# Reordered DMA issues and scatter calls in a cross-attention and mixture-of-experts kernel on one Trainium2 core

## The chip, the cores and the metric

The kernel runs on one core of one Trainium2 chip. The metric is the device time of one execution in microseconds (us); lower is better. The engines of the core run beside each other, each its own list of instructions: TensorE (PE) multiplies, VectorE (DVE), ScalarE (ACT) and GpSimd (POOL) work element by element, and SyncE (SP) issues most of the DMA transfers. Waits between them are semaphores.

## The reference, cut to what matters

```python
def reference(x, ctx, Wq, bq, Wk, bk, Wv, bv, Wo, bo, W_experts, b_experts, W_router, b_router):
    # x: (4, 2048, 512), ctx: (4, 154, 512), 16 heads of 32, 8 experts, the best 2 used
    h = layernorm(x)
    q, k, v = h @ Wq.T + bq, ctx @ Wk.T + bk, ctx @ Wv.T + bv
    attn = softmax(q k^T / sqrt(32))              # per head, 154 keys
    x = x + (attn @ v) @ Wo.T + bo
    h = layernorm(x)
    w = softmax(h @ W_router.T + b_router)        # only the two largest of the 8 kept
    return x + sum_e w[e] * (h @ W_experts[e].T + b_experts[e])
```

## The kernel before, in words

The 8192 tokens are worked on in 16 blocks of 512 (`NB` is 16). For a block b the attention stage does, in this order: normalize x (`NX`), transpose it (`XT`), project the queries (`Q`), copy them into a layout by head (the restack, `RS`), multiply them with the keys to find the largest score of each row (`MX`, 11 steps, `DMX` reduces them), send that row of maxima to the copy (`MT`, `MR`), multiply again with the maxima subtracted (`ST`, 10 steps), take exponentials (`EX`), split them into a high and a low half-precision part (`PH`, `PL`), multiply with the values (`PV`, 8 steps of which the last, number 7, ends the block), normalize and transpose (`NM`, `AT`), project (`O`), add to x (`BX`, `Oe`), compute the router (`LA`, `LB`, `RB` to `RW`) and scatter the normalized rows to a table in memory sorted by expert (`S1`, or `SC` and `SD` for blocks near the end; eight scatters of 128 rows for each block). After it comes the expert stage: 135 tiles of 128 rows are loaded from that table, multiplied with the weights of one expert each, and added to the output.

The attention stage is a software pipeline that is written out by hand. Each engine has a function of one slot (`pe_slot`, `act_slot`, `dve_slot`, `pool_slot`, `sp_slot`) that calls the steps of several blocks in a fixed order; slots run one after the other, in a loop in the middle of the stage and written out at its ends. Each engine works in order: a step that waits holds up all behind it.

SP's slot for block b issues the load of x for the residual (`XR`, block b-2), the keys (`K`, one DMA), the restack (`RS`, 12 DMAs of 128 KB from the `qs` buffers to `Qst`), the values (`V`, two DMAs), a piece of expert weights to convert (`WL`), the x of block b+3 (`XA`), the converted weights' store (`WW`), the row of maxima (`MR`) and the store of the residual (`XS`, block b-2). `K` and `RS` wait until `ST` of block b-2 is done (`stp`), `V` until `PV` of block b-2 is done (`pvt`), `RS` also until the queries' low part is there (`qle`). `MX` of the block waits for the restack and for the keys:

```python
        if n == 0:
            e.wait_ge(restack[p], b.half(192, 192))
            e.wait_ge(ld_k[p], b.half(16, 16))
```

All of SP's DMAs go through one queue (q1 in the profile), ACT's through a second (q10), POOL's indirect ones through a third (q0). Several buffers share one tensor and show by its name in the trace: `qs`, `Qst`, `Pst` and part of `xnT` are pieces of `we_s`, the buffers of `XA` are pieces of `be_s`, and `xn1` and `xn2` both show as `xn`. So the restack is `we_s<-we_s` (line 1312), `XA` is `be_s<-in_x` (1284), `XR` is `xR_s<-in_x` (1333), `WL` is `wst<-in_weT` (1350). On POOL, `PL` is line 1170, `BX` line 1246, a scatter `S1` line 1260, and a scatter of `SC` or `SD` line 1250.

In ACT's part, `act_EX` for the last block (15) also starts the loads of the expert weights into `we_s` (1 MB for each expert) and of the experts' biases (`be_s`, 2 MB), as soon as the buffers that lie there are no longer in use: three experts and the biases before step 5, two more experts after step 9. The other three are issued by SP after the attention stage.

Of the kernel before, what the change touches and what calls it, by code (L numbers as in the profile page):

```python
# [110 lines left out]
def build(nc, x, ctxT, wqT, bq, wkT, bk, wvT, bv, woT, bo, weT, be, wrT, br, wo, boc, out):  # L111
# [15 lines left out]
    def hold(e):  # L127

        e.sem_inc(tick[id(e)], 1)  # L129
# [132 lines left out]
    def s_(name):  # L262
        return sem(name, a)
# [22 lines left out]
    stp, exd, phd, pldp, pldd = s_("stp"), s_("exd"), s_("phd"), s_("pldp"), s_("pldd")  # L286
    pvt, rcd, nmd = s_("pvt"), s_("rcd"), s_("nmd")
# [606 lines left out]
    def load_experts(e, first, last):  # L894

        if last == NE:
            e.wait_ge(pvt, 8 * NB)
        e.wait_ge(st_we, 32 * last)
        for n in range(first, last):
            e.dma_start(we_s[:, n * WN:(n + 1) * WN], we_d[n].rearrange("p l k n -> p (l k n)")).then_inc(ld_ew, 16)  # L900

    def act_EX(e, b, n):
        if b.last and n == 5:
            e.wait_ge(qp, 4 * NB)
            e.wait_ge(lap, NB)
            e.wait_ge(restack[(NB - 1) % 2], 192 * NB // 2)
            e.wait_ge(stp, 10 * (NB - 1))
            e.wait_ge(nap[0], NJ * NB)
            load_experts(e, 0, 3)
            e.dma_start(be_s[:, :], be.rearrange("(a e) n -> a (e n)", a=1).broadcast_to([P, NE * D])).then_inc(ld_ew, 16)  # L910
        e.wait_ge(stp, b.at(10, n + 1))
        h = BANK[f"ST{n}"] - 2
        at = S[:, 2 * h:2 * h + 2, :]
        if n in PLP:
            i = PLP.index(n)
            if i >= R32 or b.past(1):
                e.wait_ge(pldp, b.at(NP, i - R32 + 1 if i >= R32 else (NP - 1 - i) // R32 * R32 + i - NP + 1))
            e.activation(P32[i % R32][:, :, :], at, ACT.Exp, scale=1.0 / (SS * ROOT)).then_inc(exd, 1)  # L918
        else:
            e.activation(at, at, ACT.Exp, scale=1.0 / (SS * ROOT)).then_inc(exd, 1)  # L920
        if b.last and n == 9:
            load_experts(e, 3, 5)
# [244 lines left out]
    def pool_PL(e, b, n):  # L1167
        e.wait_ge(phd, b.at(10, n + 1))
        r = 2 * (n % 5)
        e.tensor_tensor(Pst[1][:, r:r + 2, :], exps(n), Pst[0][:, r:r + 2, :], ALU.subtract).then_inc(pldp, 1)  # L1170
# [82 lines left out]
    def pool_S1(e, b, n):  # L1253
        p, k, j = b.par, n // NJ, n % NJ
        if n == 0:
            e.wait_ge(ridx, b.at(1, 1))
            e.wait_ge(rwd, b.at(RWD, RWD))
            e.wait_ge(nap[1], b.at(NJ, NJ))
            hold(e)
        e.indirect_dma_start(xs_d.ap(), bass.IndirectOffsetOnAxis(ap=idx[p][:, n:n + 1], axis=0),  # L1260
                             xn2[p][:, j, :], None).then_inc(scat[p][k], 16)
# [21 lines left out]
            hold(e)  # L1283
        e.dma_start(xA[b.par][:, :, :], blk_rows(x, b)).then_inc(ld_xA[b.par], 16)

    def sp_K(e, b):
        p = b.par
        if b.past(2):
            e.wait_ge(stp, b.at(10, -10))
            hold(e)  # L1290
        bt = b.c // 4 if b.reg is None else (b.reg * 2 + b.c) // 4
        if b.first:
            e.wait_ge(p_kd, 16 * 12)
        e.dma_start(Kst[p][0:96, :, :].rearrange("p (g G) c -> p g (G c)", g=4), k_d[:, :, bass.ds(bt, 1), :].rearrange("p g o n -> p (g o) n")).then_inc(ld_k[p], 16)

    def sp_V(e, b):
        bt = b.c // 4 if b.reg is None else (b.reg * 2 + b.c) // 4
        if b.past(2):
            e.wait_ge(pvt, b.at(8, -8))
            hold(e)  # L1300
            sp_values(e, b, bt)

    def sp_values(e, b, bt):
# [10 lines left out]
    def sp_RS(e, b):  # L1314
        if b.reg is None and b.c == 1:
            wait_values_stored(e)
        e.wait_ge(qle, b.at(4, 4))
        hold(e)
        if b.past(2):
            e.wait_ge(stp, b.at(10, -10))  # L1320
            hold(e)
        restack_heads(e, b, (0, 1) if b.first else range(4))
# [30 lines left out]
    def sp_WW(e, b):  # L1353
        e.wait_ge(wel, b.at(1, 1))
        hold(e)
        e.dma_start(we_d[bass.ds(expert_of(b), 1), :, :, 2 * (b.c % 2):2 * (b.c % 2) + 2, :].rearrange("o p l k n -> (o p) l (k n)"),
                    wsp[:, :, :]).then_inc(st_we, 16)
# [307 lines left out]
    def pool_slot(e, s):  # L1665
        bm2, bm1, b, bp1, bp2, bp4 = s + (-2), s + (-1), s, s + 1, s + 2, s + 4
        on_bm2, on_bm1, on_b, on_bp1, on_bp2, on_bp4 = bm2.here(), bm1.here(), b.here(), bp1.here(), bp2.here(), bp4.here()
        early1, early2 = on_bm1 and bm1.here(EARLY - 2), on_bm2 and bm2.here(EARLY - 2)
        if on_bp1:
            pool_PL(e, bp1, 2)  # L1670
        if early2:
            pool_S1(e, bm2, 4)
        if on_bm1 and not bm1.last:
            pool_RP(e, bm1)
        if on_bp1:
            pool_PL(e, bp1, 3)
        if on_b:
            pool_BX(e, b, 0)
        if on_bp1:
            pool_RC(e, bp1)  # L1680
        if on_b:
            pool_BX(e, b, 1)
        if early2:
            pool_S1(e, bm2, 5)
        if on_b:
            pool_BX(e, b, 2)
        if on_bm1 and not bm1.last:
            pool_RW(e, bm1)
        if on_bp1:
            pool_PL(e, bp1, 5)  # L1690
        if early2:
            pool_S1(e, bm2, 6)
        if on_bp4:
            pool_NC(e, bp4, 0)
        if early2:
            pool_S1(e, bm2, 7)
        if on_bp1:
            pool_PL(e, bp1, 7)
        if early1:
            pool_S1(e, bm1, 0)  # L1700
        if on_bp1:
            pool_PL(e, bp1, 8)
        if early1:
            pool_S1(e, bm1, 1)
        elif on_bm1 and bm1.here(NB - 3):
            pool_SC(e, bm1)
        if on_b:
            pool_BX(e, b, 3)
        if early1:
            pool_S1(e, bm1, 2)  # L1710
        if on_b and not b.last:
            pool_NC(e, b, 1)
            pool_RQ(e, b)
        if early1:
            pool_S1(e, bm1, 3)
        elif on_bm1 and bm1.here(NB - 3):
            pool_SD(e, bm1)
        if on_bp2:
            pool_PL(e, bp2, 0)

    def sp_slot(e, s):
        bm2, b, bp1, bp3 = s + (-2), s, s + 1, s + 3
        on_bm2, on_b, on_bp1, on_bp3 = bm2.here(), b.here(), bp1.here(), bp3.here()
        if on_bm2 and not bm2.last:
            sp_XR(e, bm2)
        if on_b:
            sp_K(e, b)
            sp_RS(e, b)
            sp_V(e, b)
        if on_bp1:  # L1730
            sp_WL(e, bp1)
        if on_bp3 and bp3.past(3):
            sp_XA(e, bp3)
        if on_b:
            sp_WW(e, b)
            sp_MR(e, b)
        if on_bm2 and not bm2.last:
            sp_XS(e, bm2)
# [381 lines left out]
```

## Time and profile before

| what | value |
|---|---|
| median of 3 runs | 1271.63 us (1269.0 to 1271.68) |
| time of the profiled execution | 1271.68 us |
| its span in the trace | 1270.0 us |
| mean granted TensorE clock | 0.977 of full speed |
| PE busy | 94% of the span |
| DVE, ACT, POOL busy | 69%, 56%, 59% |
| DMA | 239.19 MB, mean 188 GB/s |

The span is what the trace covers; the execution's time is 1.7 us more. Busy shares are averages over two stages with different limits: the attention stage lasts until about 830 us, the expert stage from there to the end. In rows of the trace the first number is a start in us after the span's start, the second a duration in us.

### The profile page before, as it was taken

How to read it: one execution, taken by the hardware profiler on the slowest of the kernel's cores; microseconds unless marked ns; L12 is line 12 of the kernel's file. 1: busy time of each engine (PE TensorE's matmuls, PEld its weight loads, DVE VectorE, ACT ScalarE, POOL GpSimd, SP SyncE). 2: the span in 40 equal slices, each digit the busy share in tenths (PEclk: the TensorE clock that was granted, in tenths of full speed). 3: DMA queues.
4: the chain of work that ended last, by engine and by line, in shares of the span. 5: the costliest groups of instructions: out<-in, count | busy, mean ns of one | idle time of the engine just before them, and what ended most of it. 6: DMA issues, size and time to landing. Idle time of an engine off the chain costs nothing. (4 is left out here: it accounts for less than half of the span.)

```text
span 1270.0 us, 35737 instructions
## 1 busy us (share of the span) xinstructions
PE 1192.7 (94%) x11024; PEld 719.1 (57%) x11025; DVE 873.1 (69%) x1933; ACT 717.4 (56%) x1040; POOL 745.0 (59%) x980
## 2 busy tenths in 40 slices
PE   7977999999999999999999988689899999999997
PEld 4444666666666666666666654444455555555554
DVE  3666798889888888988987876445455555555554
ACT  4327757966976786697687547233333333343333
POOL 4004337767866866776786578655645454554445
PEclk9979999999999999999999989789999999999999
DMA  9754535855765675586557448868999999898886
GB/s 249 223 166 119 142 127 159 245 168 188 229 197 191 197 223 184 173 255 181 194 170 219 153 140 303 312 151 206 200 178 177 176 189 180 168 183 165 159 165 127
DMA packets 135544, 239.19 MB, mean 188 GB/s; under 512 B 18439, under 2 KB 49415, under 8 KB 134279
## 3 DMA queue, kind: packets, MB, share of 16 engines
q1 hardware_dynamic: 102503, 161.24, 43.0%
q0 software_dynamic: 29808, 67.73, 26.4%
q10 hardware_dynamic: 3120, 8.68, 2.0%
q8 instruction: 76, 1.25, 0.4%
q14 instruction: 37, 0.30, 0.1%
HBM read 112.00 MB, written 101.40 MB: 168 GB/s over the span
## 5 line engine op out<-in xcount | busy, mean ns | idle before, releaser
L1902 PE MATMUL S<-we_s,wq_s 128*128 x1620 | 375.3, 382 | 13.2 <-DVE wq_s L1858 5.6
L1830 POOL DMA_INDIRECT out<-xn,to x135 | 208.8, 1547 | 209.4 <-DMA out<-xn,to 135.6
L1902 PEld LDWEIGHTS S<-we_s,wq_s 128*128 128x128 f16 x1620 | 157.6, 98 | 180.7 <-issue 21.8
L1170 POOL TENSOR_TENSOR we_s<-P_s,we_s 128x1024 f16<-128x1024 f32 x96 | 204.7, 2134 | 93.6 <-ACT we_s L936 92.8
L1841 ACT ACTIVATE wq_s<-PVp 128x512 f16<-128x512 f32 x137 | 81.6, 597 | 269.2 <-PE PVp L1892 243.7
L984 DVE TENSOR_REDUCE mx_sb<-S 128x6 f32<-128x924 f32 x160 | 171.4, 1112 | 11.9 <-PE S L726 8.9
L1880 DVE SCALAR_TENSOR_TENSOR att<-S,be_s 128x512 f32<-128x512 f32 x135 | 93.4, 692 | 108.8 <-PE S L1902 100.6
L746 PE MATMUL W<-wo_s,aT_hi 128*128 128x512 f16 x512 | 164.8, 384 | 3.0 <-issue 1.7
L708 PE MATMUL W<-we_s,wq_s 128*128 128x512 f16 x512 | 160.0, 384 | 4.4 <-DVE xnT_lo L962 3.6
L1858 DVE TENSOR_TENSOR wq_s<-PVp,wq_s 128x512 f16<-128x512 f32 x137 | 94.6, 691 | 39.1 <-ACT wq_s L1841 32.4
L818 PE MATMUL PVp<-Vm,we_s 128*128 128x33 f16 x3072 | 118.7, 178 | 0.2
L1260 POOL DMA_INDIRECT dispatched<-xn,idx x96 | 98.9, 1030 | 21.6 <-issue 19.9
L936 ACT ACTIVATE we_s<-P_s 128x1024 f16<-128x1024 f32 x96 | 102.2, 1065 | 8.6 <-PE PVp L818 4.7
L726 PE MATMUL S<-Kst,we_s 96*128 96x154 f16 x1024 | 99.3, 233 | 7.6 <-DVE mx_sb L984 5.3
L818 PEld LDWEIGHTS PVp<-Vm,we_s 128*128 128x128 f16 x3072 | 106.0, 97 | 0.4 <-issue 0.4
L726 PEld LDWEIGHTS S<-Kst,we_s 96*128 96x128 f16 x1024 | 78.8, 99 | 46.0 <-DVE mx_sb L984 8.0
L1094 DVE TENSOR_TENSOR we_s<-S,we_s 128x1024 f16<-128x1024 f32 x64 | 78.1, 1220 | 36.6 <-ACT we_s L936 36.6
L1848 ACT ACTIVATE xn<-att,wt 128x512 f32<-128x512 f32 x135 | 96.3, 713 | 9.8 <-DVE att L1880 3.8
L918 ACT ACTIVATE P_s<-S 128x1024 f32<-128x1024 f32 x96 | 98.4, 1025 | 2.4 <-PE S L786 2.4
L746 PE MATMUL W<-wo_s,aT_lo 128*128 128x512 f16 x256 | 98.4, 384 | 0.0
L708 PE MATMUL W<-xnT_lo,wq_s 128*128 128x512 f16 x256 | 98.2, 384 | 0.0
L815 PE MATMUL PVp<-Vr,we_s 128*128 128x132 f16 x768 | 87.3, 223 | 3.6 <-DVE att L1088 2.9
(208 smaller groups left out, 2000.5 us busy)
## 6 DMA issues: line engine op xcount, KB each, us to landing
P_s<-dispatched SPq DMA_DIRECT2D x139, 260.5 KB
we_s<-we_s SPq DMA_DIRECT2D x186, 128.0 KB
be_s<-in_x SPq DMA_DIRECT2D x16, 1024.0 KB
xR_s<-in_x SPq DMA_DIRECT2D x16, 1024.0 KB, 8.1
out<-xR_s SPq DMA_DIRECT2D x16, 1024.0 KB
wst<-in_weT SPq DMA_DIRECT2D x16, 512.0 KB, 5.4
we_scratch<-wsp SPq DMA_DIRECT2D x16, 512.0 KB
Kst<-k_scratch SPq DMA_DIRECT2D x16, 480.0 KB, 10.0
```

Source lines behind the costliest of these rows:

```text
L708: m = e.matmul(W[:, bank, :], wq_s[:, wp, k, G * P:(G + 1) * P], xnT[xp][:, k, :], start=(n == 0), stop=(n == 11))
L726: m = e.matmul(S[:, 2 * (BANK[f"MX{n}"] - 2) + u % 6 // 3, (u % 3) * C:(u % 3 + 1) * C], Qst[p][0:96, h, j * P:(j + 1) * P], Kst[p][0:96, ...
L746: m = e.matmul(W[:, bank, :], aT[ap][:, k, j * P:(j + 1) * P], wo_s[:, wp, k, :], start=(n == 0), stop=(n == 11))
L818: m = e.matmul(o[:, g * 33:(g + 1) * 33], Pst[pp][:, (5 * G + g) % 10, tok], Vm[p][:, 4 * G + g, vv, :], start=False, stop=True, skip_grou ...
L918: e.activation(P32[i % R32][:, :, :], at, ACT.Exp, scale=1.0 / (SS * ROOT)).then_inc(exd, 1)
L936: e.activation(Pst[0][:, r:r + 2, :], exps(n), ACT.Copy).then_inc(phd, 1)
L984: e.tensor_reduce(mx_sb[:, 6 * n:6 * n + 6].rearrange("p (a k) -> p a k", a=2), S[:, 2 * h:2 * h + 2, 0:3 * C].rearrange("p a (k c) -> p a ...
L1170: e.tensor_tensor(Pst[1][:, r:r + 2, :], exps(n), Pst[0][:, r:r + 2, :], ALU.subtract).then_inc(pldp, 1)
L1260: e.indirect_dma_start(xs_d.ap(), bass.IndirectOffsetOnAxis(ap=idx[p][:, n:n + 1], axis=0), xn2[p][:, j, :], None).then_inc(scat[p][k], 16)
L1830: e.indirect_dma_start(out, bass.IndirectOffsetOnAxis(ap=to[u][:, :], axis=0), yw[u % YW], None, bounds_check=N - 1, oob_is_err=False, com ...
L1848: e.activation(yw[u % YW], yb[u % 2], ACT.Copy, scale=wt[u][:, 0:1]).then_inc(ywd, 1)
L1902: m = e.matmul(Yp[:, u % 2, :], gT[u % 2][xp][:, k, :], we_s[:, bass.ds(n * WN + (wp * KC + k) * D, D)], start=(c == 0), stop=(c == 11))
```

## The change

Three things are changed, and no arithmetic. On ACT, the loads of three experts and of the biases for the last block are issued before step 0 of `EX` instead of step 5. On SP, the keys' load is joined with the values' load in one function that waits for `PV` of block b-2, and the restack is issued after the loads `WL` and `XA` instead of before the values' load. On POOL, `PL` 8 comes ahead of the first scatter of block b-1, the next scatters each move back by one step, and the last of the four comes after `PL` 0.

```diff
     def act_EX(e, b, n):
-        if b.last and n == 5:
+        if b.last and n == 0:
             e.wait_ge(qp, 4 * NB)
             e.wait_ge(lap, NB)
             e.wait_ge(restack[(NB - 1) % 2], 192 * NB // 2)
...
-    def sp_K(e, b):
+    def sp_KV(e, b):
         p = b.par
         if b.past(2):
-            e.wait_ge(stp, b.at(10, -10))
+            e.wait_ge(pvt, b.at(8, -8))
             hold(e)
...
-
-    def sp_V(e, b):
-        bt = b.c // 4 if b.reg is None else (b.reg * 2 + b.c) // 4
         if b.past(2):
-            e.wait_ge(pvt, b.at(8, -8))
-            hold(e)
             sp_values(e, b, bt)
...
         if on_bp1:
             pool_PL(e, bp1, 7)
+            pool_PL(e, bp1, 8)
         if early1:
             pool_S1(e, bm1, 0)
-        if on_bp1:
-            pool_PL(e, bp1, 8)
+        elif on_bm1 and bm1.here(NB - 3):
+            pool_SC(e, bm1)
+        if on_b:
+            pool_BX(e, b, 3)
         if early1:
             pool_S1(e, bm1, 1)
-        elif on_bm1 and bm1.here(NB - 3):
-            pool_SC(e, bm1)
-        if on_b:
-            pool_BX(e, b, 3)
-        if early1:
-            pool_S1(e, bm1, 2)
         if on_b and not b.last:
             pool_NC(e, b, 1)
             pool_RQ(e, b)
         if early1:
-            pool_S1(e, bm1, 3)
+            pool_S1(e, bm1, 2)
         elif on_bm1 and bm1.here(NB - 3):
             pool_SD(e, bm1)
         if on_bp2:
             pool_PL(e, bp2, 0)
+        if early1:
+            pool_S1(e, bm1, 3)
...
         if on_b:
-            sp_K(e, b)
-            sp_RS(e, b)
-            sp_V(e, b)
+            sp_KV(e, b)
         if on_bp1:
             sp_WL(e, bp1)
         if on_bp3 and bp3.past(3):
             sp_XA(e, bp3)
         if on_b:
+            sp_RS(e, b)
             sp_WW(e, b)
             sp_MR(e, b)
```

## Rows read from the trace of the kernel before

**Rows 1.** Windows: stretch, length, busy of each engine (instructions), PE clock, DMA share, GB/s.
```profile
140.00:726.00 586.00, 580.95 (x7100) 379.92 (x7098) 504.47 (x1025) 435.70 (x606) 410.06 (x618) 1.00 0.63 191
```
**Rows 2.** Waits of PE from 140 to 726 us: total us, times, longest.
```profile
PE W L678 <- DVE aT_lo L962: 4.8, 13, 0.4
```
**Rows 3.** Timeline of SP's DMA issues in one slot: start, us, issue.
```profile
358.58 0.41 SPq L1341 DMA_DIRECT2D out<-xR_s  x1
...
360.18 1.03 SPq L1294 DMA_DIRECT2D Kst<-k_scratch  x1
...
368.21 8.41 SPq L1312 DMA_DIRECT2D we_s<-we_s  x12
...
378.86 0.38 SPq L1284 DMA_DIRECT2D be_s<-in_x  x1
```
**Rows 4.** Timeline of PE, same slot: end of `PV` 7, first `MX`.
```profile
367.31 0.46 PE L818 MATMUL PVp<-Vm,we_s 128*128 128x33 f16 x12
...
386.28 0.57 PE L726 MATMUL S<-Kst,we_s 96*128 96x154 f16 x6
```
**Rows 5.** DMA view, 357 to 373 us: KB each, us from issue to landing.
```profile
Kst<-k_scratch SPq DMA_DIRECT2D x1, 480.0 KB, 9.9
...
we_s<-mT SPq DMA_DIRECT2D x1, 16.0 KB, 2.2
```
**Rows 6.** DMA view, 376 to 392 us.
```profile
be_s<-in_x SPq DMA_DIRECT2D x1, 1024.0 KB
wst<-in_weT SPq DMA_DIRECT2D x1, 512.0 KB, 5.2
...
Vm<-vm_scratch SPq DMA_DIRECT2D x1, 264.0 KB
```
**Rows 7.** Windows of DMA rates: loads and stores; loads; two restack stretches.
```profile
360.00:368.00 8.00, 8.00 (x109) 4.99 (x106) 6.07 (x14) 6.72 (x10) 4.52 (x9) 1.00 1.03 318
384.00:388.00 4.00, 4.00 (x29) 2.23 (x28) 3.91 (x5) 3.95 (x7) 3.19 (x7) 1.00 0.98 371
60.00:66.00 6.00, 3.92 (x16) 1.83 (x14) 5.86 (x8) 1.08 (x2) 0.00 (x0) 1.00 1.11 222
146.00:152.00 6.00, 5.63 (x82) 3.95 (x81) 3.12 (x5) 6.00 (x9) 3.83 (x3) 1.00 0.83 198
```
**Rows 8.** Timeline of POOL in the slot of Rows 3.
```profile
364.94 2.12 POOL L1170 TENSOR_TENSOR we_s<-P_s,we_s 128x1024 f16<-128x1024 f32 x1 [1.16 <-ACT we_s L936]
...
371.22 0.98 POOL L1260 DMA_INDIRECT dispatched<-xn,idx  x1 [0.15 <-issue]
...
378.80 1.06 POOL L1260 DMA_INDIRECT dispatched<-xn,idx  x1 [0.15 <-issue]
```
**Rows 9.** DMA view, 762 to 776 us: POOL's queue, with four scatters.
```profile
q0 software_dynamic: 320, 1.07, 19.7%
```
**Rows 10.** Timeline of PE around its wait at 745 us.
```profile
745.10 0.57 PE L726 MATMUL S<-Kst,we_s 96*128 96x154 f16 x6 [2.28 <-DVE we_s L1094]
...
747.15 0.95 PE L726 MATMUL S<-Kst,we_s 96*128 96x154 f16 x6 [0.42 <-DVE mx_sb L984]
```
**Rows 11.** Timelines of SP, ACT, POOL and PE near the stage's end.
```profile
763.13 0.39 SPq L1333 DMA_DIRECT2D xR_s<-in_x  x1
...
776.46 0.35 ACTq L900 DMA_DIRECT2D we_s<-we_scratch  x1
...
780.32 1.28 POOL L1246 TENSOR_TENSOR xR_s<-xR_s,bo_b 128x512 f32<-128x512 f32 x1
...
792.35 0.37 SPq L1333 DMA_DIRECT2D xR_s<-in_x  x1
...
800.18 0.28 PE L850 MATMUL W<-wx_s,aT_hi 128*128 128x16 f16 x4 [4.84 <-DVE xR_s L996]
```
**Rows 12.** DMA view, 791 to 796 us: queue, packets, MB, share of 16 engines.
```profile
q10 hardware_dynamic: 276, 2.05, 100.1%
q1 hardware_dynamic: 2, 0.00, 1.1%
```

More of the change, by code:

```diff
@@ L1698, in pool_slot @@
             pool_PL(e, bp1, 7)
+            pool_PL(e, bp1, 8)
         if early1:
             pool_S1(e, bm1, 0)
-        if on_bp1:
-            pool_PL(e, bp1, 8)
-        if early1:
-            pool_S1(e, bm1, 1)
         elif on_bm1 and bm1.here(NB - 3):
@@ L1709, in pool_slot @@
         if early1:
-            pool_S1(e, bm1, 2)
+            pool_S1(e, bm1, 1)
         if on_b and not b.last:
```

## The prediction

> **What bounds the kernel now.** I read the windows first, because the shares of the page mix two stages. In the middle of the attention stage, from 140 to 726 us, PE is busy for 580.95 of 586 us [rows 1], at its full clock. The waits of PE in this stretch name the rest: 13 waits for one and the same thing, 4.8 us together, 0.37 each [rows 2]. Thirteen in 586 us means that one slot takes 45 us and has a single gap of 0.4 us. So PE's own list is the bound there; whatever the change does for POOL, SP or the DMA queues can win at most 4.8 us in this stretch, and only if it reaches the low part of the transposed attention, which DVE makes and which no edit touches. The other direction is open: any new wait of PE is paid in full, once for each slot. Then I read the timelines of SP, PE and POOL side by side in one slot, to see how late each thing arrives that PE needs [rows 3 to 5, 8], and last the end of the stage, where PE does have gaps.
>
> The slot shown is that of block 7; those of blocks 2 to 14 repeat it with the same distance, 18.07 us, between SP's first restack issue and PE's first `MX` (368.21 and 386.28) [rows 3, 4].
>
> **SP: the restack goes behind four loads.** Before, the keys' load goes out at 360.18, early, and the restack at 368.21, as soon as the queries are ready; its 12 issues take 8.41 us [rows 3]. The values, `WL` and `XA` follow it. DMAs of one queue are worked off in the order of issue as far as this trace shows: `WL`, issued just behind the restack, lands 5.2 us after its issue [rows 6], so at 383.3, and the restack is in before it, at least 3 us ahead of `MX`.
>
> After, the keys wait for `PV` 7 of block b-2. That step ends at 367.31 + 0.46 = 367.77 [rows 4], so I put the keys' issue at 367.95, near the old time of the restack. Behind them come two loads of values, `WL` and `XA`, and then the restack. The issue itself costs little: the old row of V, V, `WL` and `XA` ends at 379.24, 2.6 us after the restack's last issue at 376.62 [rows 3]; with 1.03 for the keys the restack is issued from about 371.6 to 380.1, 6 us ahead of `MX`. What counts is the data in front of it. The sizes are 480, 264, 264, 512 and 1024 KB [rows 5, 6] (the second load of values is as large as the first), 2.60 MB together.
>
> How long do 2.60 MB take? By chance the trace has the same amount in one run: the store of the residual issued at 358.58, `XR` behind it and the keys' load at 360.18 which lands 9.9 later, at 370.1 [rows 3, 5] are 1024 + 1024 + 480 KB = 2.59 MB. They take 11.5 us from first issue to landing, and one scatter went between them. Four scatters are 1.07 MB and 19.7% of 14 us, 0.69 us of the DMA engines each [rows 9]. That leaves 10.8 us. From the other side: a small transfer takes 2.2 us [rows 5], and at the best rate near by, 371 GB/s [rows 7], 2.60 MB add 7.0, in all 9.2 us. At the 318 GB/s of 360 to 368 us [rows 7] it is 10.4.
>
> Behind it the restack, 12 x 128 KB = 1.57 MB. Where both SP and ACT issued restacks and the DMA engines were full, it ran at 222 GB/s [rows 7]: 7.1 us. Where SP's issue alone limited it the rate was 198 at a DMA share of 0.83 [rows 7]; full engines would give 239 GB/s and 6.6 us.
>
> Two of POOL's scatters fall in between, those of 371.22 and 378.80 [rows 8]: 1.4 us. The scatter that the change moves behind `PL` 0 comes at about 364.94 + 2.12 = 367.1, and its data run in the 1.3 us before the keys' data start; I take nothing for it, 0.7 at worst.
>
> Sum: 367.95 + 10.8 + 1.4 + 6.6 or 7.1 = 386.75 or 387.25, against `MX` at 386.28. PE would wait 0.5 to 1.0 us, say 0.7. With the lower bound of each term, 367.95 + 9.2 + 1.4 + 6.6 = 385.15, it waits not at all and has 1.1 us left; with the upper, 387.25 + 0.7, it waits 1.7. I take the 10.8, because that row is of the same size, the same queue, and has all fixed parts in it.
>
> In which blocks? `XA` exists up to block 12 (it loads block b+3 of 15), and POOL's scatters are in these places from block 4 on. Blocks 2 and 3 lack the 1.4 us of scatters, blocks 13 and 14 the 3.3 us of 1.05 MB at 318 GB/s, block 15 also `WL`. All of these end ahead of `MX`. Blocks 0 and 1 have no earlier `PV` to wait for, so there the loads go out before the queries are ready. Nine blocks are left: 9 x 0.7 = 6.3 us. PE has no slack to win it back, since it has only the one gap of 0.37 us a slot, and that one moves along with PE.
>
> What else waits behind? `WW` and `MR` are issued after the restack, at about 380 as before, and `MR` comes only after `MX` and `MT`. `WL`, `XA` and the values land earlier than before; nobody waits for them now, and so nobody gains.
>
> **POOL: the order of scatters.** `PL` 8 comes forward by one scatter and `PL` 0 too, 1.0 us each [rows 8]. PE does not wait for `PL` between 140 and 726 us [rows 2], so this wins 0. The work that hides it is PE's own; with that cover gone it would be about 1 us a slot. The scatters themselves come one or two steps later, and the next reader of their buffers comes a slot later: 0. From block 12 on the order of `SC`, `SD` and `PL` stays what it was.
>
> **ACT: five megabytes earlier.** Three experts and the biases (3 x 1 MB + 2 MB, 5.24 MB) are issued at 776.46 now [rows 11] and would be issued at about 763, since ACT has nothing in front of `EX` 0 but the wait for `ST`. ACT's own cost is four issues (the first takes 0.35 us [rows 11]), made while it waits for `ST`. What is late next: PE stands for 4.84 us before 800.18, for DVE's `Oe` [rows 11], which needs POOL's last `BX` of block 14, the fourth of a row that begins at 780.32. So a transfer matters here only if it holds up POOL, and the one that could is `XR` of block 14, issued at 763.13 [rows 11] and needed by the first `BX` at 780.32. In order of issue it is in front of most of the new loads: even behind three of them, 2.1 + 3.15 MB at 371 GB/s are 14.2 us, so it lands by 763.13 + 2.2 + 14.2 = 779.5. I take 0. The gain is 0 as well: the first expert tile starts after the last `O`, and the experts that SP loads afterwards are the later ones in both kernels.
>
> How queues share the DMA engines is seen at 791 to 796 us: `XR` of block 15 was issued on q1 at 792.35 [rows 11], yet q10, with the loads that ACT had issued before, had 100.1% of the engines and q1 1.1% [rows 12]. The older transfer went first.
>
> The Trainium skill says otherwise ("DMA: Bandwidth & Descriptors", section Queues, rings and completion order): each DMA engine takes turns between the queues that have work, a packet at a time. This trace does not agree, by the 100.1% against 1.1%. By that rule the sum would have the cost of the second rival below; by the rows it has none.
>
> **Sum.** 1271.68 (the profiled execution; the median of the runs shown is 1271.63, practically the same) + 6.3 = 1278.0 us.
>
> **The rivals.** A change of 0.2%, 2.5 us, is about what a measurement of this kernel can tell from no change.
>
> First, the restack is just in time: the loads run at 371 GB/s, as at 384 to 388 us [rows 7], and PE waits less than 0.28 us in each of nine blocks. Then the time is 1271.7 to 1274. For it speaks that the lower bounds leave 1.1 us; against it the measured 10.8 us for a like chain. Chance 0.30.
>
> Second, the 5.24 MB of ACT hold up `XR` of block 14. If ACT's queue goes mostly first, XR and the store in front of it, 2.1 MB, end with the 5.24 MB: at 371 GB/s 7.3 MB take 19.8 us, which is 763.13 + 2.2 + 19.8 = 785.1. POOL is 4.8 us late from 780.32 on, and so is PE at 800.18: with the body in time 1276.5, with the stalls 1283. Alone, chance 0.06.
>
> Third, the restack is so late that the clock falls. After a wait of 2.28 us PE's group of six `MX` products took 0.95 us instead of 0.57 [rows 10]: half clock for a while, some 3 us more. It decides from a wait of about 2 us: nine times (2 + 3) is 45 us. It needs all upper bounds and something more, for example the moved scatter in the wrong place. A wait of 1.3 to 2 us without the clock gives 12 to 18. Together 0.08, mostly the milder form, 1284 to 1290.
>
> Fourth, faster. The one place with something to win is the end of the stage, where PE idles 4.84 us at 800.18 and some more around it. If the full DMA engines there (q10 at 100.1% [rows 12]) slow POOL or the signals, and the earlier loads take this away, 3 to 6 us could come back, and the body would have to be in time: 1266 to 1269. It decides from a saving of 2.5 us in POOL's row up to `BX`. Against it: what PE waits for there is DVE and POOL, not a DMA. Chance 0.14, with both kinds of luck together.
>
> **How the numbers follow.** Forecast (a wait of 0.3 to 1.3 us in nine blocks, 2.7 to 12 us) 0.42; in time 0.30; `XR` late 0.06; much later restack 0.08; faster 0.14. Slower by over 0.2% is 0.42 + 0.06 + 0.08 = 0.56, within 0.2% 0.30, faster 0.14. The likeliest case's own range is 1274.4 to 1284. The range for 8 in 10 goes from 1269 (it leaves out most of the faster case) to 1287 (it leaves out the worse part of the third rival).
>
> **What would show it.** Right: in the waits of PE a row of L726 for DMA `we_s`, nine times, 0.3 to 1.3 us, in the slots of blocks 4 to 12 and not in those of 2, 3, 13 and 14; the keys issued 0.2 us after `PV` 7 and the restack from 3.5 us later; a slot longer by the same amount. The wait of 0.37 us for DVE stays. Wrong: no such row and a slot as before (rival one); POOL's first `BX` of block 14 waiting for DMA `xR_s` (rival two); the wait at 800.18 shorter than 4 us (rival four). The prediction falls if the DMA engines take 2.60 MB of loads in less than about 10 us here, or if the restack runs faster than 239 GB/s when it is queued.

## The result and the profile after

The changed kernel took 1305.88 us (median of 4 runs, 1305.13 to 1308.86), the kernel before 1270.41 beside it: ratio 1.0284, 95% interval 1.0263 to 1.0306. That is 35.5 us slower where 6.3 were forecast, and above the range of 1269 to 1287. Ratios here and below leave out two executions in a slower state (1297.07 us with SP's part alone, 1974.82 with POOL's order). The profiled execution has a span of 1304.8 us at a mean clock of 0.973.

Windows of the changed kernel, as in [rows 1]:
```profile
140.00:726.00 586.00, 560.93 (x6779) 363.19 (x6777) 487.89 (x991) 421.91 (x588) 394.22 (x599) 0.99 0.61 185
```
The waits of PE in the same stretch, as in [rows 2]:
```profile
PE W L678 <- DVE aT_lo L962: 12.8, 13, 1.1
PE S L726 <- DMA we_s<-we_s: 12.1, 9, 2.3
```
PE is busy for 20.0 us less than in [rows 1], and the two rows name them: 12.8 + 12.1 - 4.8 = 20.1. The second is the one I had forecast, nine times, in the slots of blocks 4 to 12 and in no other, but twice as large. The first is the old gap of 0.37 us: it still has that in the slots of blocks 2 and 3 and is 1.1 us in the eleven after them. I had written that it stays.

The slot of block 7, timelines of SP, POOL, PE and ACT, to be laid beside [rows 3, 4, 8]. In the changed kernel the restack is line 1307:
```profile
376.24 0.65 SPq L1294 DMA_DIRECT2D Kst<-k_scratch  x1
...
379.93 11.39 SPq L1307 DMA_DIRECT2D we_s<-we_s  x12
```
```profile
372.31 2.12 POOL L1170 TENSOR_TENSOR we_s<-P_s,we_s 128x1024 f16<-128x1024 f32 x1 [0.93 <-ACT we_s L936]
374.60 0.99 POOL L1260 DMA_INDIRECT dispatched<-xn,idx  x1 [0.16 <-issue]
```
```profile
374.68 0.46 PE L818 MATMUL PVp<-Vm,we_s 128*128 128x33 f16 x12
...
378.39 0.63 PE L678 MATMUL W<-ident,att 128*128 128x128 f32 x4 [1.07 <-DVE aT_lo L962]
...
396.53 0.57 PE L726 MATMUL S<-Kst,we_s 96*128 96x154 f16 x6 [2.01 <-DMA we_s<-we_s]
```
```profile
375.98 1.06 ACT L936 ACTIVATE we_s<-P_s 128x1024 f16<-128x1024 f32 x1 [0.87 <-PE PVp L818]
```
The last matmul of `PV` 7 ends at 375.14. ACT and SP, which both wait for its signal, go on at 375.98 and 376.24, 0.84 and 1.10 us later. In the slot of block 2, where no scatter stands there, SP issued the keys at 142.80, 0.09 us after `PV` 7 had ended. What ACT does late is a `PH`; behind it in its list is `ATh`, on it hangs DVE's `aT_lo`, and on that PE's 1.07. The scatter moved behind `PL` 0 runs from 374.60 to 375.59, over the moment of the signal.

The clock. Timeline of PE, two slots of the changed kernel:
```profile
300.78 0.57 PE L726 MATMUL S<-Kst,we_s 96*128 96x154 f16 x6 [2.13 <-DMA we_s<-we_s]
332.08 0.63 PE L678 MATMUL W<-ident,att 128*128 128x128 f32 x4 [1.09 <-DVE aT_lo L962]
...
348.86 0.57 PE L726 MATMUL S<-Kst,we_s 96*128 96x154 f16 x6 [0.66 <-DMA we_s<-we_s]
378.39 0.63 PE L678 MATMUL W<-ident,att 128*128 128x128 f32 x4 [1.07 <-DVE aT_lo L962]
```
After a wait of 2.13 us PE needs 31.30 us from `MX` to `AT`, after one of 0.66 us 29.53. Three slots waited over 2 us, 3 x 1.77 = 5.3 us. In one of them the windows show the granted clock fall to half, the lower of its two levels (1.2 of 2.4 GHz):
```profile
494.00:496.00 2.00, 2.00 (x11) 1.18 (x10) 0.92 (x1) 0.50 (x1) 1.96 (x2) 0.50 0.35 133
```
12.1 + (12.8 - 4.8) + 5.3 = 25.4 us, and one more slot, after 726 us, adds 0.8. The group of `ST` that PE starts at 763.96 in the trace of before starts at 789.82 here, 25.9 later. The rest comes behind it. Timelines of POOL and PE at the stage's end, beside [rows 11]:
```profile
813.21 1.26 POOL L1246 TENSOR_TENSOR xR_s<-xR_s,bo_b 128x512 f32<-128x512 f32 x1 [6.85 <-DMA xR_s<-in_x]
```
```profile
817.10 1.46 PE L786 MATMUL S<-we_s,Kst 97*128 97x512 f16 x3 [6.51 <-DVE we_s L1094]
...
832.80 0.26 PE L850 MATMUL W<-wx_s,aT_hi 128*128 128x16 f16 x4 [0.97 <-DVE xR_s L996]
```
POOL stands 6.85 us for `XR` of block 14, which was issued at 788.99 and so took 24 us; PE gets a wait of 6.51 us, and the old one of 4.84 shrinks to 0.97. At 832.80 the changed kernel is 32.6 us behind the row at 800.18 of [rows 11], where it was 25.9 behind before this place. Of these 6.7 us the waits are 6.51 - (4.84 - 0.97) = 2.6. The rest goes mainly with the clock: behind the wait of 6.51 us it was granted at half in the windows from 817 to 823 us, for instance
```profile
821.00:823.00 2.00, 2.00 (x6) 0.76 (x5) 0.00 (x0) 2.00 (x4) 2.00 (x2) 0.50 0.99 418
```
The last 2 us of the 34.8 by which the spans differ come in the expert stage and are not looked into.

### The profile page after: what moved, and what is told of

It is laid out like the page before. It is cut to its first block and busy times, and to the rows that moved or that the text cites. A ratio compares the mean times of both kernels' runs of the same rounds, so it can differ in the third digit from the quotient of the medians.

```text
span 1304.8 us, 35723 instructions
## 1 busy us (share of the span) xinstructions
PE 1203.3 (92%) x11024; PEld 719.3 (55%) x11025; DVE 877.2 (67%) x1933; ACT 716.5 (55%) x1040; POOL 745.7 (57%) x980
## 3 DMA queue, kind: packets, MB, share of 16 engines
q8 instruction: 76, 1.25, 0.4%
## 5 line engine op out<-in xcount | busy, mean ns | idle before, releaser
L708 PE MATMUL W<-we_s,wq_s 128*128 128x512 f16 x512 | 163.5, 392 | 4.2 <-DVE xnT_lo L962 3.4
L726 PE MATMUL S<-Kst,we_s 96*128 96x154 f16 x1024 | 100.3, 234 | 20.5 <-DMA we_s<-we_s 12.1
L597 POOL TENSOR_SCALAR nrm<-aggr 128x4 f32<-128x4 f32 x32 | 7.1, 222 | 166.3 <-ACT nrm L582 165.3
```

What stands on the lines that cost most here:

```text
L708: m = e.matmul(W[:, bank, :], wq_s[:, wp, k, G * P:(G + 1) * P], xnT[xp][:, k, :], start=(n == 0), stop=(n == 11))
L726: m = e.matmul(S[:, 2 * (BANK[f"MX{n}"] - 2) + u % 6 // 3, (u % 3) * C:(u % 3 + 1) * C], Qst[p][0:96, h, j * P:(j + 1) * P], Kst[p][0:96, ...
```

## The experiments

There were eighteen runs on four chips, each beside the kernel before on the same chip: the first chip had four runs (kernel before 1269.5 us), the second eight (1260.7 for four of them, 1261.6 for the other four), the third four (1269.7), the fourth two (1262.2). That turned out to be half of the answer. Which chip gave the result itself is not on record; it was like the first (kernel before 1270.4, late signals in the trace). A cost in us in this part is the ratio less one, times the kernel before; for the result that makes 36.1 us. "The parts" below are those of the diff ahead of the prediction.

### One part at a time, first chip

**ACT's part alone** (`n == 5` to `n == 0`).

> The kernel before with only ACT's edit: the loads of three experts and of the biases go out before step 0 of EX of the last block instead of step 5. Theory (three separate causes): XR of block 14 lands some 20 us after its issue, POOL's first BX of block 14 waits for it, PE waits 6 to 7 us once for ST 8 of block 15, and the whole is 6 to 9 us slower than before; no wait in the body. Rival (the body's stalls carry the loss, the end is only shifted): within 3 us of before.

Measured: 1.0032 (1.0015 to 1.0049), 4.1 us. The waits of the body are those of [rows 2]. POOL's timeline:
```profile
788.29 1.26 POOL L1246 TENSOR_TENSOR xR_s<-xR_s,bo_b 128x512 f32<-128x512 f32 x1 [7.04 <-DMA xR_s<-in_x]
```
The second rival's mechanism is there, with a price between the two expectations: DVE's `Oe` waits for this `BX`, PE waits 5.9 us for DVE, and the wait of 4.84 has shrunk to 1.0.

**SP's part alone** (`sp_KV`, and `RS` behind `XA`).

> The kernel before with only SP's edit: keys joined with values behind PV 7, restack behind WL and XA. Theory (the restack's lateness needs both the data in front of it and the scatter that POOL's edit moves): the first MX waits less than in the changed kernel, 0 to 0.8 us in nine slots against 1.35 on average, the wait for the low part of AT stays 0.37, and the time is 0 to 8 us above before. Rival (SP's edit alone makes the whole wait for the restack): 12 us of waits for the restack and some 18 us slower with the slow clock behind them.

Measured: 1.0066 (1.0043 to 1.0089), 8.4 us. Waits of PE, 140 to 726 us, and the slot of block 7:
```profile
PE S L726 <- DMA we_s<-we_s: 8.8, 10, 1.8
PE W L678 <- DVE aT_lo L962: 4.8, 13, 0.4
```
```profile
371.73 0.65 SPq L1294 DMA_DIRECT2D Kst<-k_scratch  x1
...
375.20 11.75 SPq L1307 DMA_DIRECT2D we_s<-we_s  x12
```
```profile
391.23 0.57 PE L726 MATMUL S<-Kst,we_s 96*128 96x154 f16 x6 [1.11 <-DMA we_s<-we_s]
```
This is the forecast's case: the keys 0.29 us after `PV` 7 had ended at 371.44, and waits of 0.5 to 1.8 us in the slots of blocks 4 to 12, 0.95 on average, with one of 0.18 in that of block 2. From the keys' issue to the restack's landing 19.5 us went, where I had 18.8 to 19.3.

**POOL's part alone.**

> The kernel before with only POOL's edit. Theory: the scatter that now follows PL 0 runs while PE ends PV 7, and the signal of PV 7 reaches the engines 0.8 us late, so PE's wait for the low part of AT grows from 0.37 to 1.1 us in 11 slots: 8 us slower, no wait for the restack. Rival (the longer wait for AT comes from the keys' and values' loads at that moment, not from POOL): no change, within 1 us.

Measured: 1.007 (1.005 to 1.0091), 8.9 us. I had costed it at nothing. Waits of PE and, in one slot, POOL, PE and ACT:
```profile
PE W L678 <- DVE aT_lo L962: 12.9, 13, 1.2
```
```profile
367.46 0.99 POOL L1260 DMA_INDIRECT dispatched<-xn,idx  x1 [0.16 <-issue]
```
```profile
367.54 0.46 PE L818 MATMUL PVp<-Vm,we_s 128*128 128x33 f16 x12
```
```profile
368.87 1.06 ACT L936 ACTIVATE we_s<-P_s 128x1024 f16<-128x1024 f32 x1 [0.89 <-PE PVp L818]
```
`PV` 7 ends at 368.00, the scatter at 368.45, and ACT gets the signal at 368.87. So all of the new waits for `aT_lo` are of this part. The slots of blocks 2 and 3 are a check inside the run: their `PL` steps have moved as well, but they have no scatters, and their wait stays at 0.37 us. So it is the scatters and not the place of `PL`.

**SP's and POOL's parts together.**

> SP's and POOL's edits together, without ACT's, that is the changed kernel with the loads at step 5 again. Theory: the body as in the changed kernel, 26 us slower than before, the end as before: 1296 to 1298 us. Rival (ACT's edit has no own cost): 1305 us. If SP's and POOL's edits alone add up to clearly less than this, they work on each other.

Measured: 1.0216 (1.0152 to 1.0279), 27.4 us, with 13.0 us of waits for the restack in nine slots and 12.7 for `aT_lo`. Alone they cost 8.4 and 8.9, together 10 more. ACT's 4.1 on top give 31.5; the whole change measured 36.1 in its own comparison. (The 27.4 is itself uncertain by 8 us either way, so the 10 more are barely shown.)

### Pieces of the parts, second chip

**The keys joined with the values only; the restack directly behind them.**
```diff
         if on_b:
-            sp_K(e, b)
-            sp_RS(e, b)
-            sp_V(e, b)
+            sp_KV(e, b)
+            sp_RS(e, b)
```


> SP's edit in part: keys joined with the values behind PV 7, then the restack at once, WL and XA behind it as before. In front of the restack are 1.0 MB instead of 2.6. Theory (the data in front of the restack make it late): the restack lands over 4 us earlier than with the full edit and MX never waits: within 2 us of before. Rival (the wait on PV 7 and the keys' place make it late): waits of MX for the restack or the keys as with the full edit.

Measured: 1.0005 (0.9987 to 1.0023), no wait for the restack.

**The restack behind V, `WL` and `XA` only; the keys early as before.**
```diff
             sp_K(e, b)
-            sp_RS(e, b)
             sp_V(e, b)
...
         if on_b:
+            sp_RS(e, b)
             sp_WW(e, b)
```


> SP's edit in the other part: the keys' load stays early with its old wait, only the restack goes behind the values, WL and XA. In front of it are 2.1 MB instead of 2.6. Theory: 1.5 us less data in front than with the full edit, so MX waits less or not: 0 to 3 us above before. Rival (the place of the restack behind XA is all that counts): as slow as the full edit of SP.

Measured: 1.0016 (0.9999 to 1.0032), one wait of 0.8 us. So neither half of SP's part costs by itself on this chip: with 1.0 MB in front of the restack it lands in time, with 2.1 MB in time but for one slot. SP's whole part alone was not run here; with 2.6 MB in front and POOL's order the restack is late here too (the run with both parts, below).

**Only the fourth scatter behind `PL` 0.**
```diff
-        if early1:
-            pool_S1(e, bm1, 3)
...
             pool_PL(e, bp2, 0)
+        if early1:
+            pool_S1(e, bm1, 3)
```


> POOL's edit in part: only the fourth scatter is moved behind PL 0, PL 8 and the other scatters stay. Theory (this scatter delays the signal of PV 7): the wait for the low part of AT is 1.1 us in 11 slots, some 8 us slower, all of POOL's loss. Rival (PL 8's place or the others): within 1 us of before.

Measured: 0.9992 (0.9972 to 1.0013), waits for `aT_lo` 4.8 us in all, 0.37 each. The scatter starts at the same moment against `PV` 7 as on the first chip, and the signal is in time. I took my theory for fallen.

**POOL's part, but the fourth scatter ahead of `PL` 0.**

> POOL's edit in the other part: PL 8 comes first and the scatters move back by one step, but the fourth stays ahead of PL 0. Theory: within 1 us of before, with the wait of 0.37 us for AT unchanged. Rival: some 8 us slower.

Measured: 1.0015 (1.0002 to 1.0028), waits 0.37 us. From these two I read that it needs both scatters in their new places. That was wrong: I compared across chips.

**POOL's part, with the fourth scatter behind `PL` 2.**

> The POOL edit alone, but the fourth scatter comes a step later still, behind PL 2, 3 us after the last step of PV has ended (the third keeps its new place). Theory A (a scatter that is issued just while PV 7 ends, with the scatter before it only 4.6 us ahead, makes the signal of PV 7 come 0.9 us late): the wait of PE for aT_lo is 0.37 us again in every slot and the time is that of the kernel before within 0.2%. Theory B (POOL itself is late, whatever the moment): the wait stays at 1.1 us and the ratio is about 1.007. Theory C (it is a matter of the order in the queue, so that the lateness follows the scatter): another wait of PE for ACT or POOL of about 0.7 us shows behind the new place, ratio 1.005 or so.

Measured: 1.009 (1.0058 to 1.0123). No late signal, but a new row in the waits of PE:
```profile
PE W L678 <- DVE xR_s L996: 7.1, 11, 0.7
```
Two scatters now stand in a row in front of `BX`, DVE's `Oe` waits for that, and PE for `Oe`, 0.65 us in each of eleven slots. It is theory C's size by another mechanism: simply one scatter more of POOL's time at a place where POOL is the one that is waited for. The second chip, as it turned out, has no late signals at all, so this run tests none of the three theories of them.

**SP's and POOL's parts, but the fourth scatter ahead of `PL` 0.**

> The changed kernel without its ACT edit and with the fourth scatter ahead of PL 0, so that the signal of PV 7 should be in time. Theory A (the two edits add more than their parts because the late signal also holds back SP's issue of the keys and with it the restack, until waits over 2 us bring the clock down): the wait for aT_lo is 0.37, the waits for the restack are those of the SP edit alone or a little more, 9 us in ten slots, and the ratio is 1.007 to 1.010. Rival (the restack is held up by the scatters' own data and places): the waits for the restack stay at 12 to 13 us and the ratio is 1.012 to 1.016.

Measured: 1.0116 (1.0082 to 1.015). The waits of PE:
```profile
PE S L726 <- DMA we_s<-we_s: 13.0, 9, 2.5
PE W L678 <- DVE aT_lo L962: 4.8, 13, 0.4
```
The waits are the rival's, and the ratio lies just under its range: without any late signal the restack makes PE wait 13.0 us, as much as with it on the first chip. That doesn't show that the scatters' places take the 8.8 us of SP's part to 13, since the 8.8 are of another chip, and SP's part alone was not run on this one. In two of the slots the wait was over 2 us, and only one of them paid for it: after 2.51 us PE needed 30.50 us from `MX` to `AT`, after 2.08 us 28.83, like after short waits, and the clock was granted in full.

**The whole change, but `XA` behind the restack.**
```diff
+        if on_b:
+            sp_RS(e, b)
         if on_bp3 and bp3.past(3):
             sp_XA(e, bp3)
         if on_b:
-            sp_RS(e, b)
             sp_WW(e, b)
```


> The whole changed kernel, but XA (1.05 MB) is issued behind the restack. Theory A (it is the data in front of the restack that count): 3.3 us less in front, so no wait for the restack is left, nor the slow clock; what remains is the wait for aT_lo, 13 times 1.1 us, and the end of the stage: 4 + 9 = 13 us, ratio about 1.010. Rival (the late keys or the place behind them is enough): waits of L726 of 0.5 us or more stay in most slots, ratio 1.015 or more.

Measured: 1.0046 (1.0023 to 1.0069), and of PE's waits from 140 to 726 us only the old row is left:
```profile
PE W L678 <- DVE aT_lo L962: 4.8, 13, 0.4
```
Laid beside the 13.0 us of the run before it on the same chip: with 1.05 MB less in front nobody waits for the restack, so the data in front of it are what counts. At the stage's end ACT's part is at work here as on the first chip, by POOL's wait:
```profile
782.78 1.26 POOL L1246 TENSOR_TENSOR xR_s<-xR_s,bo_b 128x512 f32<-128x512 f32 x1 [7.10 <-DMA xR_s<-in_x]
```
But the expected 1.1 us waits for `aT_lo` were missing too, although the scatters stood as in the changed kernel. That made me look at what the two chips have in common and what not.

**ACT's part with one expert only before step 0**, the rest at step 5.

> The ACT edit cut down: only one expert (1.05 MB of the 5.24 MB) is loaded before step 0, the rest at step 5 as before. Theory A (the 5.24 MB on ACT's queue go ahead of XR of block 14, which was issued before most of them, and POOL's first BX is late by what is left): XR lands in time, no wait of POOL for xR_s, time that of the kernel before within 0.2%. Rival (any load of ACT at this place holds XR up by its full length, because the queue of SP hardly gets a turn): XR lands only after the one expert and the wait of PE grows by 1 us or more, 1.001 to 1.002; or the cost comes from ACT's own wait and issue, then the 4.1 us of the full edit stay.

Measured: 1.0003 (0.9983 to 1.0022); POOL waits for no `xR_s` and PE's 4.84 at the old place is back. With all 5.24 MB at this place POOL had waited 7.10 us on this same chip. So it is the amount on ACT's queue, not the place nor ACT's wait and its first issue.

### The same kernels on other chips

**A place in the stage's end, third chip.** `BX` 3 of the last blocks goes ahead of the four scatters of `SC`.
```diff
-        elif on_bm1 and bm1.here(NB - 3):
-            pool_SC(e, bm1)
         if on_b:
             pool_BX(e, b, 3)
+        if not early1 and on_bm1 and bm1.here(NB - 3):
+            pool_SC(e, bm1)
```


> The kernel before with one step moved, on POOL in the slots of the last blocks: BX 3 goes ahead of the four scatters of SC. PE waits 4.84 us at 800.18 for DVE's Oe, which needs that BX. Theory: with BX 3 some 5 us earlier, this wait is gone or below 1 us, and the time is 3 to 4.8 us less, ratio 0.996 to 0.998. Rival: the scatters of block 13 or 14 come later by 1.3 us, and what waits for them (the first tiles of the expert stage) takes it back, or PE waits at the next place instead: ratio 0.999 to 1.001.

Measured: 0.9996 (0.9978 to 1.0013). The wait for `Oe` is gone, and PE waits elsewhere, among others 2.09 us at 759.61 for the reduction of `MX`. No version here beats the kernel before by more than can be measured.

**SP's part again, third chip.**

> The SP edit alone, the same kernel as before in this study. If this is the chip of the eight later runs (kernel before at 1261 us): theory A (data and scatters' places alone make the waits for the restack) expects 8 to 9 us in ten slots again, ratio 1.006; the rival (part of them comes from the late signal, by which the keys go out) expects 5 us or less. If it is the first chip: 8.8 us and 1.0066 again.

Measured: 1.0113 (1.0098 to 1.0129), 14.3 us; waits for the restack 11.9 us in nine slots, up to 2.2 us. In the slot of block 7 the chain from the keys' issue to `MX` took 20.2 us (371.44 to 391.60), against 19.5 on the first chip. In this slot the same kernel differs by 0.7 us, over the nine slots of blocks 4 to 12 by 0.45 on average. Within one execution this stretch varies more, from 19.0 to 20.6.

**POOL's part again, third chip.**

> The POOL edit alone, the same kernel as before in this study. If this is the chip of the eight later runs: theory A (the lateness is that of the first chip, for signals that fall beside a scatter) expects waits for aT_lo of 0.37 us, 4.8 to 5.6 in all, and the kernel before's time within 0.2%; the rival (this order of steps makes the signal late on any chip) expects 1.1 us thirteen times and 1.007. If it is the first chip: 12.9 us and 1.007 again.

Measured: 1.007 (1.0053 to 1.0087), waits for `aT_lo` 12.9 us: as on the first chip.

**The whole change again, third chip.**

> The changed kernel itself, once more. If this is the chip of the eight later runs: theory A expects no wait for aT_lo over 0.4 us, waits for the restack of 12 to 13 us in nine slots with some at low clock as in the run with SP's edit and the fourth scatter ahead of PL 0 (1.0116), and ACT's 4 us on top: ratio 1.013 to 1.018. The rival (the late signal is in the order itself) expects 1.028 with waits for aT_lo of 1.1 us. If it is the first chip: 1.028 again.

Measured: 1.0222 (1.0199 to 1.0245), 28.2 us, with 14.9 us of waits for the restack and 12.8 for `aT_lo`. The parts on this chip are 14.3 + 8.9, and ACT's 4.1 from the first makes 27.3: here the parts add up to the whole within the noise.

These two runs also show, on one chip, what the late signal does to the wait for the restack. In the slot of block 7 of SP's part alone, `PV` 7 ended at 371.15, the keys went out at 371.44 and `MX` was due at 391.60 - 1.76 = 389.84. In the whole change the three are 379.98, 381.11 and 401.04 - 1.65 = 399.39. The keys go out 0.84 us later against `PV` 7, but `MX` is due 0.72 later, since PE has waited that much longer for `aT_lo`. That leaves 0.1 us of this slot's wait for the restack to the late keys.

**The fourth scatter alone, and POOL's part, both on the fourth chip.**

> The kernel before with only the fourth scatter moved behind PL 0, as run before on the chip without late signals. If this chip has late signals: theory A (a PE signal is late where a scatter has just started, and only that) expects the waits for aT_lo at 1.1 us in eleven to thirteen slots, 12 to 13 us in all, and a ratio of 1.005 to 1.008, as much as the whole POOL edit; the rival (the third scatter's new place is needed as well) expects 0.37 us and 1.000. If it has none: 0.37 us and 0.999 again.

> The POOL edit alone. If this chip has late signals: 12.9 us of waits for aT_lo and 1.007, as twice before. If it has none: theory A (the order of steps costs nothing by itself) expects waits of 0.37 us, 4.8 to 5.6 in all, and a ratio of 0.999 to 1.002; the rival (the order itself makes the wait) expects 1.1 us and 1.007.

Measured: 0.9997 (0.9979 to 1.0014) and 1.0004 (0.9978 to 1.003). The waits for `aT_lo` are 0.37 us in both. One slot of POOL's part alone on this chip, POOL, PE and ACT, to be laid beside the same three rows of the first chip:
```profile
364.06 0.99 POOL L1260 DMA_INDIRECT dispatched<-xn,idx  x1 [0.16 <-issue]
```
```profile
364.13 0.46 PE L818 MATMUL PVp<-Vm,we_s 128*128 128x33 f16 x12
```
```profile
364.62 1.06 ACT L936 ACTIVATE we_s<-P_s 128x1024 f16<-128x1024 f32 x1
```
The scatter starts 0.53 us before the end of `PV` 7, as there, and ACT goes on at 364.62, with no wait. The kernel is the same, so the lateness is not the kernel's but the chip's. POOL's part costs 8.9 us on the first and on the third chip, and nothing on the fourth. Not run: the fourth scatter alone on a chip with late signals. That this scatter is the one that does it there is argued from its place in the rows: where only SP's part runs, on the same chips, no scatter stands over the end of `PV` 7 in these slots, and the signal is in time.

The kernel before had shown it all along, at the end of its stage. ACT, POOL and PE around 770 us in the profiled execution of the kernel before (1270.0 us), rows that I had not used:
```profile
772.85 1.06 ACT L936 ACTIVATE we_s<-P_s 128x1024 f16<-128x1024 f32 x1 [2.60 <-remote]
```
```profile
766.86 1.08 POOL L1250 DMA_INDIRECT dispatched<-xn,idx  x1 [0.63 <-issue]
...
770.78 0.96 POOL L1250 DMA_INDIRECT dispatched<-xn,idx  x1 [0.30 <-issue]
```
```profile
768.76 0.46 PE L818 MATMUL PVp<-Vm,we_s 128*128 128x33 f16 x12
```
And the same step on the fourth chip (the kernel with the fourth scatter moved; these four are not touched by it):
```profile
767.25 1.06 ACT L936 ACTIVATE we_s<-P_s 128x1024 f16<-128x1024 f32 x1 [0.16 <-PE PVp L818]
```
```profile
763.64 1.08 POOL L1250 DMA_INDIRECT dispatched<-xn,idx  x1 [0.63 <-issue]
...
767.56 0.96 POOL L1250 DMA_INDIRECT dispatched<-xn,idx  x1 [0.30 <-issue]
```
```profile
766.70 0.46 PE L818 MATMUL PVp<-Vm,we_s 128*128 128x33 f16 x12
```
In the first, `PV` ends at 769.22 in a row of four scatters, and ACT gets the signal at 772.85, 3.6 us later and after the last of them; in the second it comes 0.09 us after 767.16, with the last scatter still to start. Each of the profiles of the first and third chip has this lateness at this place, of 2.2 to 3.8 us.

## Why the prediction was wrong, step by step

**That PE is the bound of the body and has 4.8 us to win, and that any new wait is paid in full:** right. The 20.1 us of new waits are missing in PE's 20.0.

**SP's part, 0.7 us in nine slots:** the mechanism, the blocks and the kind of row were right; the size was off. In the slot of block 7 of the changed kernel the forecast's terms read so. The keys go out 1.10 us after `PV` 7, not 0.18: 0.92 more. From their issue to the landing it takes 20.3 us (376.24 to 396.53), where the middle of my terms is 10.8 + 1.4 + 6.85 = 19.05: 1.25 more. `MX` itself would come 0.87 later, since `PV` 7 to `MX` is 19.38 us (375.14 to 396.53 - 2.01) instead of 18.51 [rows 4]. 0.7 + 0.92 + 1.25 - 0.87 = 2.0, the 2.01 of the row. The mis-sized term is the time behind the keys' issue: SP's twelve issues took 11.39 us here, where I had kept the 8.41 of [rows 3], and how the 1.25 divides between loads and restack these rows don't show. Where only this part runs, the waits are 8.8 us, near the 6.3; on the third chip 11.9. The 19.05 was within the spread of single slots (18.8 to 21.2 us in the profiles with this part), but below their middle. That XA's megabyte decides, as the sum says, is shown by the run with `XA` behind the restack.

**The keys' issue at + 0.18, POOL's part at nothing, and the wait of 0.37 that "stays":** this is the step that failed. I took for granted that a signal of PE arrives 0.1 to 0.2 us after the matmuls, because it does in the slot that I read, and asked of the moved scatter only where its data go. On the chip of the profile it makes the signal of `PV` 7 0.8 us late: 8.0 us in the body through ACT and `aT_lo`. It also sends the keys out late, the 0.92 above, but nearly all of that is given back by the 0.87: `MX` is itself due later (0.84 against 0.72 in the two runs of the third chip). So its cost is in the waits for `aT_lo` and not in those for the restack.

**The clock:** the third rival was right in its mechanism ([rows 10] as the analog) and near in its threshold, given a chance of 0.08. Three waits over 2 us cost 5.3 us, 1.77 each where I had put some 3. Over all the profiles with SP's part, nine waits of 1.98 to 2.92 us were followed by such a loss; one of 2.08 us was not, nor those of 1.93 us and less. It did not need "the moved scatter in the wrong place", as I wrote: SP's part alone on the third chip had a wait of 2.23 us, and the run with the fourth scatter put back one of 2.51, both with the loss.

**ACT's part at nothing:** wrong; the second rival was right. I had read [rows 12] as "the older transfer went first". But they need not show a contest. Here `XR` was issued right behind ACT's first load and took 24 us. In the DMA view of the changed kernel from 789 to 813 us, queue, packets, MB and share:
```profile
q10 hardware_dynamic: 576, 5.24, 54.0%
q1 hardware_dynamic: 1063, 2.10, 26.2%
```
q1's 2.10 MB, the store and `XR`, were done only with q10's 5.24 MB: not in order of issue, but beside each other. How they shared shows in the part of it in which both had work, 792 to 810 us:
```profile
q10 hardware_dynamic: 556, 5.19, 70.8%
q1 hardware_dynamic: 558, 1.11, 16.3%
```
The two moved the same number of packets. But one of q10 carried 9.3 KB on average and one of q1 2.0 KB, so q1 moved about a fifth of q10's bytes. I had the price, 4.8 us, without the slow clock behind the wait, and measured 4.1 alone, and 6.7 at this place of the changed kernel's profile. The Trainium skill's rule ("DMA: Bandwidth & Descriptors", section Queues, rings and completion order), that each DMA engine takes turns between its queues a packet at a time, which I had set aside, agrees with the 556 packets against 558. The two rows of [rows 12] may not be against it. `XR` was issued there at 792.35, and its first packets ran between 795 and 796 us. Here ACT's first load was issued at 788.77 and its first packets ran between 791 and 792. If a transfer's data begin that late, most of the 5 us of [rows 12] lay before `XR` had anything to move; that it was held back is the other reading, and the rows don't separate the two.

**The sum:** 8.4 + 8.9 + 4.1 = 21.4 us by the parts on the first chip, 27.3 on the third; the whole was 36.1 and 28.2. On the third chip nothing is left over. On the first, taking the result's chip for one like it, some 15 us are, against an interval of 8 us either way for SP's and POOL's parts together. What can be seen of them is that the restack was later than with SP's part alone (13.0 and 12.1 against 8.8 us of waits), with two and three slots slow by the clock against none, and that `XR`'s wait costs more by the clock than its length. On the third chip the waits were 14.9 against 11.9 us. Whether POOL's new order makes the restack that much later, or the slots' own spread does, stays open; its scatters' data near the restack are a candidate that no run isolates.

On a chip without late signals, the whole change was not run. SP's and POOL's parts with the fourth scatter put back cost 1.0116 there, which with ACT's 4 us would make about 1.015, some 19 us by this estimate: on the 1271.7 of the forecast that is 1290, outside my range, but the interval reaches into it.

## What to carry to other kernels

A moved instruction can cost more than its own time and data: look in the trace for the nearest place where the same kind already stands beside a signal (here, four scatters beside a `PV`), and read how late the waiting engines go on. Before a transfer is put behind others in its queue, add up what is in front of it against the due time with the worst row, and then ask what a wait does to the clock. And compare kernels only with the kernel before on the same chip: a theory fell here, and rose again, because two kernels were compared across chips.

## What the runs showed of the hardware

Chips of two kinds. On the first and third, signals of PE that fall beside a scatter on POOL mostly arrive 0.7 to 1.0 us late at ACT (2.2 to 3.8 us in a row of four), and those with no scatter beside them within 0.3 us; on the second and fourth all do, beside a scatter too. The kernel before takes 1269.5 and 1269.7 us on the former, 1260.7 to 1262.2 on the latter. What the chips differ in is open, and so is most of the 8 us: up to the first tile of the expert stage the kernel before is only 2.9 us later (819.87) than the run with one expert on the second chip (817.02). A wait for it looks like a wait for PE, and once like one for "remote", although PE had long ended.

A queue does not keep its place against another: 1.05 MB issued right behind the first of 5.24 MB on another queue landed after 24 us, and with 1.05 MB there instead of 5.24 in time. While both had work they moved packet for packet, 556 and 558, and the queue with packets of 2.0 KB got 1.11 MB against 5.19 for the one with 9.3 KB.

PE's clock, in the profiles with SP's part: nine waits for the restack of 1.98 to 2.92 us were followed by a granted clock at the lower level and 1.5 to 1.8 us more until `AT`; one of 2.08 us and all up to 1.93 us were not.

SP's twelve issues of the restack took 8.1 to 9.2 us in the slots of blocks 4 to 12 of the kernel before, 8.7 to 9.9 with 1.0 MB issued just in front of them (second chip), 9.2 to 11.0 with 1.5 MB (second chip), and 11.2 to 13.1 us with 2.6 MB (first three chips). That the backlog of the queue holds up its issuing engine is the likely reading; no run isolates it.
